# Layer 0 of a four-layer graph network: the first pair's scores ahead of the value sums, and the copy between two exponentials

## The chip, the core and the metric

The kernel runs on one core of one Trainium2 chip, in one launch. The metric is the device time in microseconds, the median of three executions. A profile of one execution, with a record of every instruction, was taken beside them. The engines are TensorE (matmuls; in the profile PE, and PEld for its weight loads), VectorE (DVE), ScalarE (ACT), GpSimd (POOL) and SyncE (SP), which issues the DMAs. Each engine works through its own instructions in order; semaphores tie them together.

## What is computed

Four layers update x (8 graphs of 1024 nodes with 128 features) one after the other. The change touches layer 0 alone, attention with 4 heads of 32 features. The 1024 keys fall into 8 chunks of 128, and each chunk has a softmax of its own:

```python
kc = k.reshape(B, H, Nc, CHUNK, Dh)
vc = v.reshape(B, H, Nc, CHUNK, Dh)
scores = jnp.einsum('bhnd,bhjcd->bhnjc', q, kc) / jnp.sqrt(jnp.asarray(Dh, dtype=q.dtype))
scores = jnp.clip(scores, -10.0, 10.0)
scores = jnp.where(mask == 0, jnp.asarray(-10.0, scores.dtype), scores)
attn = jax.nn.softmax(scores, axis=-1)
ctx = jnp.einsum('bhnjc,bhjcd->bhnd', attn, vc)
...
out = ctx @ Wo.T + bo
out = out + x
```

A layer norm and a residual follow. The input of each layer is relu(layernorm(x)). Layers 1 to 3 are other kinds of graph attention.

## The kernel before

Layer 0 runs in eight stages, one for each graph. A stage has 16 steps: two halves of 512 queries, by 8 key chunks in each (`half, jt = divmod(i, T)`). Four heads are handled in two pairs, `hp` 0 and 1. The parts of a step, by engine and by the names of the profile:

- **Scores** (`scores`, L386, and L390 in the chunks 1, 4 and 7, whose mask is added by matmuls): TensorE writes the keys x queries scores of a pair into one half of `s_ps`. It waits until the exponential has read that half (`exp_done`). There is one such buffer for each pair.
- **Exponential** (`exps`, L558): ScalarE writes a pair's exponentials to `e`. `e` has two buffers in turn, so the first exponential of step i waits for the value sums of step i-2 (`pv_done`).
- **Clip** (`clip`, L704, or L701 in the masked chunks): VectorE clips `e` in place. There are two in a step.
- **Column sums** (`sums`, L402): TensorE adds up `e` over the keys, as 32-column matmuls side by side, into `sum_ps`.
- **Value sums** (`values`, L420): TensorE multiplies `e` with the values, 4 heads side by side, into the bank `ctx_ps`. They wait for `chunk_copied` and `chunk_weighed`.
- **Copy** (`copy_chunk`, L564): ScalarE takes `ctx_ps` out into `chunk`.
- **Inverses** (`spread_inverses`, L412) and **product** (`weigh`, L725): half a stage later, TensorE spreads the inverse sums of a chunk to all rows, into the same bank `ctx_ps`, and VectorE multiplies them with the copy. Every second product is followed by an addition (L730).

So `ctx_ps` holds in turn the value sums of one chunk (written by TensorE, read by ScalarE) and the inverses of an older one (written by TensorE, read by VectorE). The order is written out by hand. At step i TensorE does: inverses of step i, column sums and value sums of step i-1, scores of step i+1. ScalarE does the copy of step i-2 and both exponentials of step i; VectorE the product, then the two clips. In between stand pieces of the next graph's projections and of the last graph's output, at fixed steps: on ScalarE, for instance, eight parts of h (L125) after step 3; on VectorE the inversion (`invert`, 2.7 us in all) between the clips of steps 0 and 8, and the residual's work after steps 2 and 14.

Stage 0 has no inverses before its step 9.

Of the kernel before, what the change touches and what calls it, by code (L numbers as in the profile page):

```python
# [177 lines left out]
def layer0(c, x_in, adj_t, w):  # L178
# [7 lines left out]
    STEPS = 2 * T  # L186
# [6 lines left out]
    with ExitStack() as ctx:  # L193
# [157 lines left out]
        def _(pe):  # L351
# [5 lines left out]
            def turn(n, par):  # L357
                if not (isinstance(n, int) and n == 0):
                    pe.wait_ge(u_ready, 2 * n - 1)
                nm.pe_turn(pe, n, par)  # L360
# [55 lines left out]
            def values(b, par, i):  # L416
                pe.wait_ge(chunk_copied, 16 * b + i + 1)
                pe.wait_ge(chunk_weighed, 16 * b + i + 1)
                for h in range(H):
                    ins = pe.matmul(ctx_ps[h * DH:(h + 1) * DH, :], v[par][:, i % T, h * DH:(h + 1) * DH],  # L420
                                    e[:, 2 * (i % 2) + h // 2, h % 2, :], start=True, stop=True,
                                    tile_position=(0, h * DH))
                ins.then_inc(pv_done, 1)
# [13 lines left out]
            def stacks(n):  # L437
                pe.wait_ge(q_stacked, STACK * (n + 1))
                pe.wait_ge(k_stacked, STACK * (n + 2))

            def stage(b, par, first, more):
                n = b + 1
                if first:
                    stacks(b)
                    for hp in range(2):
                        scores(b, par, 0, hp)
                    pe.wait_ge(v_ready, b + 1)
                for i in range(STEPS):
                    before = (b, par, i - 1) if i >= 1 else (b - 1, 1 - par, STEPS - 1)
                    after = (b, par, i + 1) if i + 1 < STEPS else (n, 1 - par, 0)  # L450
                    if first and i == 9:
                        pe.wait_ge(selected, 16)
                    if not (first and i < 9):
                        pe.wait_ge(chunk_copied, 16 * b + i)
                        spread_inverses(b, i)
                    if not (first and i == 0):
                        sums(before[0], before[2])
                        values(*before)
                    if more or i + 1 < STEPS:
                        if i + 1 == STEPS:  # L460
                            stacks(n)
                        for hp in range(2):
                            scores(*after, hp)
                    if not first and i == 1:
                        if isinstance(b, int) and b == 1:
                            pe.wait_ge(const_stored, 48)
                        output(b - 1, 0)
                    if more:
                        if i == 4:
                            turn(n, 1 - par)  # L470
                        elif i == 7:
                            q(n)
                        elif i == 9:
                            k(n)
                        elif i == 12:
                            vv(n)
                    if i == 14:
                        if more:
                            pe.wait_ge(v_ready, n + 1)
                        if not first:  # L480
                            output(b - 1, 1)

            def tail():
# [12 lines left out]
                output(B - 1, 1)  # L496

            walk(pe, prepare, stage, tail)

        @block.scalar  # L500
        def _(act):
            act.sem_inc(exp_done, 2)
            act.sem_inc(chunk_copied, 1)
            act.sem_inc(k_stacked, STACK)
            act.wait_ge(loaded, 80)

            def h_t(n):
                act.wait_ge(v_projected, n + 1)
                if not (isinstance(n, int) and n == 0):
                    act.wait_ge(x_updated, 2 * n - 1)  # L510
                nm.act_h_t(act, n)

            def high(n, projected, bias, done, free, value):
                act.wait_ge(projected, n + 1)
                act.wait_ge(free, value)
                act.activation(split[:, 0, :], aux[:, :], ACT.Identity, bias=bias[:, 0:1]).then_inc(done, 1)

            def q(n):
                high(n, q_projected, bq, q_hi, k_stacked, STACK * (n + 1))

            def k(n):
                high(n, k_projected, bk, k_hi, q_stacked, STACK * (n + 1))

            def v_out(n, par):
                act.wait_ge(v_projected, n + 2)
                act.activation(v[par][:, :, :], aux_t, ACT.Copy).then_inc(v_ready, 1)

            def normed(b, half):
                m = 2 * b + half
                act.wait_ge(offset2_done, m + 1)  # L530
                for t in range(4):
                    ins = act.activation(u[:, t, :], u[:, t, :], ACT.Identity, bias=offset2[:, t:t + 1],
                                         scale=rstd2[:, t:t + 1])
                ins.then_inc(u_normed, 1)

            def prepare(n, par):
                nm.act_h(act, n, par)
                h_t(n)
                q(n)
                k(n)  # L540
                v_out(n, par)

                act.wait_ge(prior_steps, 2)
                act.activation(pr[:, 3:4], pr[:, 2:3], ACT.Exp, scale=-1.0).then_inc(prior_ready, 1)
                act.wait_ge(late_loaded, 128)
                for x in range(16):
                    act.activation(spread[:, x // 8, x % 8, :], same_head, ACT.Copy,
                                   scale=row_is[:, x:x + 1]).then_inc(selected, 1)
                act.wait_ge(prior_ready, 1)
                act.activation(pr[:, 4:5], pr[:, 3:4], ACT.Ln, bias=c.ones[:, 0:1])  # L550
                act.activation(pr[:, 6:7], c.ones[:, 0:1], ACT.Ln, bias=pr[:, 5:6]).then_inc(prior_ready, 1)
                act.wait_ge(bounded, 3)

            def exps(b, i, hp):
                act.wait_ge(s_ready, 32 * b + 2 * i + hp + 65)
                if hp == 0:
                    act.wait_ge(pv_done, 16 * b + i + 1)
                act.activation(e[:, 2 * (i % 2) + hp, :, :], s_ps[:, hp, :, :], ACT.Exp,  # L558
                               scale=SCALE).then_inc(exp_done, 1)

            def copy_chunk(b, i):
                act.wait_ge(pv_done, 16 * b + i + 3)
                act.wait_ge(chunk_weighed, 16 * b + i + 1)
                act.activation(chunk[:, i % T, :], ctx_ps[:, :], ACT.Copy).then_inc(chunk_copied, 1)  # L564

            def stage(b, par, first, more):
                n = b + 1
                for i in range(STEPS):
                    if i >= 2:
                        copy_chunk(b, i - 2)  # L570
                    elif not first:
                        copy_chunk(b - 1, i + STEPS - 2)
                    exps(b, i, 0)
                    exps(b, i, 1)
                    if i == 0 and not (isinstance(b, int) and b < 2):
                        normed(b - 2, 1)
                    elif i == 4 and not first:
                        normed(b - 1, 0)
                    if more:
                        if i == 3:  # L580
                            if not first:
                                act.wait_ge(u_ready, 2 * b + 1)
                                act.wait_ge(late_ready, b)
                            nm.act_h(act, n, 1 - par)
                        elif i == 6:
                            h_t(n)
                        elif i == 8:
                            q(n)
                        elif i == 11:
                            k(n)  # L590
                        elif i == 13:
                            v_out(n, 1 - par)

            def tail():
                copy_chunk(B - 1, STEPS - 2)
                copy_chunk(B - 1, STEPS - 1)
                normed(B - 2, 1)
                normed(B - 1, 0)
                normed(B - 1, 1)

            act.sem_inc(pv_done, 2)
            walk(act, prepare, stage, tail)

        @block.vector
# [1411 lines left out]
```

## Time and profile before

| | |
|---|---|
| median of three executions | 2156.48 us |
| lowest and highest | 2144.48 and 2159.27 us |
| the profiled execution | 2157.34 us, of which the span of the trace 2155.5 us |
| mean granted clock of TensorE in it | 0.902 of full speed |
| busy in the span: TensorE, VectorE, ScalarE | 1736.7, 1595.2, 1346.2 us |

Layer 0 fills the span from about 57 to 749 us. Times below are microseconds from the start of the span. Matmuls are pipelined, and a row's time reaches until its last column has left; how long a group takes in a chain is the distance between its start and the start of the next. A bracket at the end of a row tells how long the engine had been idle and what it waited for. The granted clock has two levels here, 1.00 (2.4 GHz) and 0.50 (1.2 GHz).

### The profile page before, as it was taken

To read this page: it belongs to the slowest core of one execution; us is meant where nothing else is said; L and a number is where in the kernel's file an instruction comes from. 1 tells how busy PE (TensorE), PEld (TensorE's weight loads), DVE (VectorE), ACT (ScalarE), POOL (GpSimd) and SP (SyncE) were. 2 spreads that over 40 slices of the span, in tenths; PEclk is the share of its full clock that TensorE was granted. 3 is DMA by queue.
4 is the path that set the end of the run, shared out by engine and by line. 5 is a ranking of instruction groups with operands and counts; after the bars stand their busy time and mean duration, and the time that the engine had idled before them with its cause. 6 is when DMAs were issued, how large, how long until landed. Compare 5 with 4: busy or idle time off the path is not lost. (4 is left out here: it accounts for less than half of the span.)

```text
span 2155.5 us, 37200 instructions
## 1 busy us (share of the span) xinstructions
PE 1736.7 (81%) x13876; PEld 1102.1 (51%) x13876; DVE 1595.2 (74%) x2790; ACT 1346.2 (62%) x1767; POOL 111.6 (5%) x130
## 2 busy tenths in 40 slices
PE   2888888888888827699899977797877776999997
PEld 1344343443344325577677755675656553555554
DVE  2676767677767746678888889988988965767674
ACT  2665645555455517577677778988889834545553
POOL 0000000101000010000000000000000000000000
PEclk9999989999899957899999988998988988999999
DMA  6413031130311021111111112221112202000000
GB/s 191 98 40 79 1 79 40 41 79 1 79 40 40 1 82 55 35 40 50 41 40 41 50 51 70 70 70 61 61 60 70 79 26 79 11 10 20 10 10 20
DMA packets 50270, 108.92 MB, mean 51 GB/s; under 512 B 7633, under 2 KB 26450, under 8 KB 50098
## 3 DMA queue, kind: packets, MB, share of 16 engines
q1 hardware_dynamic: 50098, 106.54, 17.1%
q8 instruction: 119, 1.95, 0.4%
q14 instruction: 53, 0.43, 0.1%
HBM read 68.37 MB, written 4.59 MB: 34 GB/s over the span
## 5 line engine op out<-in xcount | busy, mean ns | idle before, releaser
L1052 ACT ACTIVATE g<-s_all,steep_d 128x1024 fp8e4<-128x1024 f32 x608 | 642.3, 1135 | 42.1 <-DMA s_all<-s_rows 26.4
L993 PE MATMUL acc<-parts,g 128*128 128x102 bf16 (+1 forms) x6144 | 418.0, 229 | 28.5 <-DVE sums L1143 19.3
L993 PEld LDWEIGHTS acc<-parts,g 128*128 128x128 fp8e4 x6144 | 401.6, 99 | 61.6 <-issue 43.8
L975 PE MATMUL post<-parts,edge 128*128 128x396 bf16 (+1 forms) x1024 | 232.9, 383 | 83.7 <-DVE base L1151 83.7
L558 ACT ACTIVATE e<-s_ps 128x1024 f32<-128x1024 f32 x256 | 248.9, 1022 | 37.0 <-PE s_ps L390 26.6
L1136 DVE TENSOR_TENSOR g<-g,edge 128x1024 int32<-128x1024 int32 x192 | 227.7, 1218 | 34.6 <-ACT g L1052 34.6
L564 ACT ACTIVATE chunk<-ctx_ps 128x512 f32<-128x512 f32 x128 | 76.2, 596 | 243.1 <-PE ctx_ps L420 243.1
L386 PE MATMUL s_ps<-qs,ks 128*128 128x512 f32 x512 | 207.4, 517 | 12.4 <-issue 7.5
L975 PEld LDWEIGHTS post<-parts,edge 128*128 128x128 fp8e4 x1024 | 102.2, 102 | 191.3 <-issue 106.6
L704 DVE SCALAR_TENSOR_TENSOR e<-e,bound 128x1024 f32<-128x1024 f32 x160 | 189.8, 1220 | 8.4 <-ACT e L558 8.4
L420 PE MATMUL ctx_ps<-e,v 128*32 128x512 f32 x1024 | 152.7, 668 | 48.8 <-DVE weighed L725 42.0
L386 PEld LDWEIGHTS s_ps<-qs,ks 128*128 128x128 f32 x512 | 102.0, 213 | 144.1 <-issue 109.1
L1830 ACT ACTIVATE z<-z,shift 128x1024 f32<-128x1024 f32 x64 | 73.6, 1150 | 160.5 <-DVE shift L1906 160.5
L1143 DVE TENSOR_REDUCE sums<-acc 128x132 f32<-128x396 f32 (+1 forms) x256 | 133.9, 566 | 28.5 <-PE acc L993 28.3
L402 PE MATMUL sum_ps<-e,pick 128*32 128x256 f32 x2048 | 146.2, 405 | 9.4 <-DVE e L704 8.8
L725 DVE TENSOR_TENSOR weighed<-chunk,ctx_ps 128x512 f32<-128x512 f32 x96 | 65.8, 686 | 96.0 <-PE ctx_ps L412 94.7
L1737 PE MATMUL s_ps<-ht,q 128*128 128x512 f32 x256 | 121.5, 597 | 4.3 <-DVE top L1899 3.2
L1899 DVE CUSTOM_DVE_ANT_0 z<-s_ps,bias 128x1024 f32<-128x1024 f32 x64 | 78.4, 1225 | 60.7 <-PE s_ps L1737 60.4
L1759 PE MATMUL o_ps<-zt,h 128*128 128x512 f32 x256 | 118.0, 605 | 6.3 <-ACT zt L1835 6.3
L125 ACT ACTIVATE h<-x,offset,rstd 128x128 f32<-128x128 f32 (+1 forms) x256 | 101.8, 482 | 31.1 <-POOL offset L118 31.1
L1126 DVE TENSOR_SCALAR g<-s_all,minus_d 128x1024 fp8e4<-128x1024 f32 x160 | 114.1, 746 | 6.0 <-DVE x L1183 2.7
L412 PE MATMUL ctx_ps<-inv_sum,spread 128*128 128x256 f32 x256 | 68.7, 352 | 48.1 <-DVE inv_sum L716 28.7
(157 smaller groups left out, 2208.8 us busy)
## 6 DMA issues: line engine op xcount, KB each, us to landing
s_all<-s_rows SPq DMA_DIRECT2D x96, 512.0 KB, 3.6
qs<-split SPq DMA_DIRECT2D x128, 128.0 KB, 2.3
ks<-split SPq DMA_DIRECT2D x128, 128.0 KB, 2.3
x<-in_x SPq DMA_DIRECT2D x8, 512.0 KB, 6.0
adj_in<-in_adj SPq DMA_DIRECT2D x8, 512.0 KB, 4.1
out_x<-x SPq DMA_DIRECT2D x8, 512.0 KB, 3.2
parts<-in_adj_t SPq DMA_DIRECT2D x6, 512.0 KB, 6.0
chunk<-in_adj_t SPq DMA_DIRECT2D x4, 512.0 KB, 6.5
```

Of the source, the lines that this page charges most:

```text
L386: ins = pe.matmul(s_ps[:, hp, j, :], ks[par][:, 2 * hp + j, jt * P:(jt + 1) * P], qs[par][:, 2 * hp + j, half * HALF:(half + 1) * HALF], s ...
L402: ins = pe.matmul(sum_ps[h * DH:(h + 1) * DH, :], pick[:, at:at + DH], e[:, 2 * (i % 2) + h // 2, h % 2, q * QUARTER:(q + 1) * QUARTER], s ...
L420: ins = pe.matmul(ctx_ps[h * DH:(h + 1) * DH, :], v[par][:, i % T, h * DH:(h + 1) * DH], e[:, 2 * (i % 2) + h // 2, h % 2, :], start=True, ...
L558: act.activation(e[:, 2 * (i % 2) + hp, :, :], s_ps[:, hp, :, :], ACT.Exp, scale=SCALE).then_inc(exp_done, 1)
L704: dve.scalar_tensor_tensor(out=tile, in0=tile, scalar=CLIP_LO, in1=lim, op0=ALU.max, op1=ALU.min).then_inc(p_ready, 1)
L975: ins = pe.matmul(self.post[:, it % 2, 0:H * 3 * W1].rearrange("p (h k c) -> p h k c", h=H, k=3), self.c.edge[:, jt, it * P:(it + 1) * P], ...
L993: ins = pe.matmul(self.acc[:, bank, o:o + self.NS], self.g[:, h % RING, jt, it * P:(it + 1) * P], self.upper[par][:, jt, h, :, :].rearrang ...
L1052: act.activation(self.g[:, h % RING, jt, :], self.s_all[:, h % 2, :], ACT.Relu, bias=self.steep_d[par][:, jt, h:h + 1], scale=STEEP, satur ...
L1136: dve.tensor_tensor(both, both, c.edge[:, some, :].rearrange("p t n -> p (t n)").bitcast(I32), ALU.bitwise_and).then_inc(self.g_ready, 1)
L1143: dve.tensor_reduce(self.sums[par][:, h, PER * k:PER * k + PER, :, :].rearrange("p i k c -> p i (k c)"), self.acc[:, (READS * h + k) % 4, ...
L1737: ins = pe.matmul(s_ps[:, j * HALF:(j + 1) * HALF], q[par][:, i * P:(i + 1) * P], ht[par][:, j * HALF:(j + 1) * HALF], start=True, stop=True)
L1759: ins = pe.matmul(o_ps[:, :], c.h[:, par, t, :], zt[:, quad, t, :], start=(t == 0), stop=(t == T - 1))
```

## The change

On TensorE, the scores of the next step are split: those of the first pair stand ahead of the value sums, those of the second behind. On ScalarE, the copy moves from the front of the first exponential to the place between the two. All instructions stay as they are, and none is added or removed; what each waits for stays too.

```diff
--- before.py
+++ after.py
@@ -455,12 +455,14 @@
                         spread_inverses(b, i)
                     if not (first and i == 0):
                         sums(before[0], before[2])
-                        values(*before)
                     if more or i + 1 < STEPS:
                         if i + 1 == STEPS:
                             stacks(n)
-                        for hp in range(2):
-                            scores(*after, hp)
+                        scores(*after, 0)
+                    if not (first and i == 0):
+                        values(*before)
+                    if more or i + 1 < STEPS:
+                        scores(*after, 1)
                     if not first and i == 1:
                         if isinstance(b, int) and b == 1:
                             pe.wait_ge(const_stored, 48)
@@ -566,11 +568,11 @@
             def stage(b, par, first, more):
                 n = b + 1
                 for i in range(STEPS):
+                    exps(b, i, 0)
                     if i >= 2:
                         copy_chunk(b, i - 2)
                     elif not first:
                         copy_chunk(b - 1, i + STEPS - 2)
-                    exps(b, i, 0)
                     exps(b, i, 1)
                     if i == 0 and not (isinstance(b, int) and b < 2):
                         normed(b - 2, 1)
```

TensorE, before: step 9 of stage 0, with the inverses (`spread`), the column sums (`sum_ps<-e,pick`), the value sums (`ctx_ps<-e,v`) and the scores (`s_ps<-qs,ks`).

```order
L412 MATMUL ctx_ps<-inv_sum,spread 128x256 [waits inverted,chunk_copied,selected]
L412 MATMUL ctx_ps<-inv_sum,spread 128x256
L402 MATMUL sum_ps<-e,pick 32x256 [waits sums_read,p_ready]
L402 MATMUL sum_ps<-e,pick 32x256 x7
L420 MATMUL ctx_ps<-e,v 32x512 [waits chunk_weighed,chunk_copied]
L420 MATMUL ctx_ps<-e,v 32x512 x3
L386 MATMUL s_ps<-qs,ks 128x512 [waits exp_done]
L386 MATMUL s_ps<-qs,ks 128x512
L386 MATMUL s_ps<-qs,ks 128x512 [waits exp_done]
L386 MATMUL s_ps<-qs,ks 128x512
```

TensorE, the same place in the changed program:

```order
L412 MATMUL ctx_ps<-inv_sum,spread 128x256 [waits inverted,chunk_copied,selected]
L412 MATMUL ctx_ps<-inv_sum,spread 128x256
L402 MATMUL sum_ps<-e,pick 32x256 [waits sums_read,p_ready]
L402 MATMUL sum_ps<-e,pick 32x256 x7
L386 MATMUL s_ps<-qs,ks 128x512 [waits exp_done]
L386 MATMUL s_ps<-qs,ks 128x512
L420 MATMUL ctx_ps<-e,v 32x512 [waits chunk_weighed,chunk_copied]
L420 MATMUL ctx_ps<-e,v 32x512 x3
L386 MATMUL s_ps<-qs,ks 128x512 [waits exp_done]
L386 MATMUL s_ps<-qs,ks 128x512
```

The two scores of the first pair have moved from behind the value sums to the front of them; their wait for `exp_done` goes with them.

ScalarE, before: steps 3 to 5 of stage 1, with the eight parts of h after step 3.

```order
L558 ACTIVATE e<-s_ps 128x1024 [waits s_ready]
L125 ACTIVATE h<-x,offset,rstd 128x128 [waits offset_done,late_ready,u_ready]
L125 ACTIVATE h<-x,offset,rstd 128x128 x7
L564 ACTIVATE chunk<-ctx_ps 128x512 [waits chunk_weighed,pv_done]
L558 ACTIVATE e<-s_ps 128x1024 [waits pv_done,s_ready]
L558 ACTIVATE e<-s_ps 128x1024 [waits s_ready]
L532 ACTIVATE h_t<-h_t,offset,rstd 128x128 [waits offset2_done]
L532 ACTIVATE h_t<-h_t,offset,rstd 128x128 x3
L564 ACTIVATE chunk<-ctx_ps 128x512 [waits chunk_weighed,pv_done]
```

ScalarE, the same place in the changed program (lines are 2 higher there):

```order
L560 ACTIVATE e<-s_ps 128x1024 [waits s_ready]
L125 ACTIVATE h<-x,offset,rstd 128x128 [waits offset_done,late_ready,u_ready]
L125 ACTIVATE h<-x,offset,rstd 128x128 x7
L560 ACTIVATE e<-s_ps 128x1024 [waits pv_done,s_ready]
L566 ACTIVATE chunk<-ctx_ps 128x512 [waits chunk_weighed,pv_done]
L560 ACTIVATE e<-s_ps 128x1024 [waits s_ready]
L534 ACTIVATE h_t<-h_t,offset,rstd 128x128 [waits offset2_done]
L534 ACTIVATE h_t<-h_t,offset,rstd 128x128 x3
L560 ACTIVATE e<-s_ps 128x1024 [waits pv_done,s_ready]
```

The copy now stands behind one exponential in each step.

## Rows read from the trace of the kernel before

**Rows 1.** Windows: busy us per engine, clock, DMA, over layer 0

```profile
57.00:749.00 692.00, 599.11 (x4448) 287.16 (x4448) 498.53 (x791) 390.63 (x518) 39.09 (x47) 0.91 0.21 47
```

**Rows 2.** Waits of layer 0 (52 to 745 us): total us, times, longest

```profile
PE ctx_ps L420 <- DVE weighed L725: 39.2, 20, 2.1
...
PE ctx_ps L412 <- ACT chunk L564: 8.1, 5, 2.8
...
PE ctx_ps L420 <- DVE ctx_sb L725: 6.6, 10, 1.1
```

**Rows 3.** Timeline of stage 3, steps 10 to 12: start, us, instruction

```profile
369.70 1.07 PE L420 MATMUL ctx_ps<-e,v 128*32 128x512 f32 x8
...
370.70 1.20 PE L386 MATMUL s_ps<-qs,ks 128*128 128x512 f32 x4
370.83 0.60 ACT L564 ACTIVATE chunk<-ctx_ps 128x512 f32<-128x512 f32 x1 [3.96 <-PE ctx_ps L420]
371.46 1.94 ACT L558 ACTIVATE e<-s_ps 128x1024 f32<-128x1024 f32 x2
...
371.73 0.39 PE L412 MATMUL ctx_ps<-inv_sum,spread 128*128 128x256 f32 x2
...
372.06 1.07 PE L402 MATMUL sum_ps<-e,pick 128*32 128x256 f32 x16
372.16 0.69 DVE L725 TENSOR_TENSOR weighed<-chunk,ctx_ps 128x512 f32<-128x512 f32 x1 [0.34 <-PE ctx_ps L412]
...
373.00 1.06 PE L420 MATMUL ctx_ps<-e,v 128*32 128x512 f32 x8
...
373.99 0.50 PE L386 MATMUL s_ps<-qs,ks 128*128 128x512 f32 x1
...
375.57 0.59 ACT L564 ACTIVATE chunk<-ctx_ps 128x512 f32<-128x512 f32 x1
...
376.21 0.50 PE L412 MATMUL ctx_ps<-inv_sum,spread 128*128 128x256 f32 x2
```

**Rows 4.** VectorE's timeline, stage 3, products 13 to 15

```profile
382.08 0.69 DVE L725 TENSOR_TENSOR weighed<-chunk,ctx_ps 128x512 f32<-128x512 f32 x1 [2.03 <-PE ctx_ps L412]
...
385.38 0.69 DVE L725 TENSOR_TENSOR weighed<-chunk,ctx_ps 128x512 f32<-128x512 f32 x1 [0.34 <-PE ctx_ps L412]
...
394.00 0.69 DVE L725 TENSOR_TENSOR weighed<-chunk,ctx_ps 128x512 f32<-128x512 f32 x1
```

**Rows 5.** Timelines of stage 1 (steps 3 to 5) and stage 4 (steps 3, 4)

```profile
146.69 1.02 ACT L558 ACTIVATE e<-s_ps 128x1024 f32<-128x1024 f32 x1
...
148.34 0.68 DVE L725 TENSOR_TENSOR weighed<-chunk,ctx_ps 128x512 f32<-128x512 f32 x1
...
149.17 1.07 PE L420 MATMUL ctx_ps<-e,v 128*32 128x512 f32 x8 [1.74 <-DVE weighed L725]
...
152.55 0.69 DVE L725 TENSOR_TENSOR weighed<-chunk,ctx_ps 128x512 f32<-128x512 f32 x1 [1.26 <-PE ctx_ps L412]
...
156.73 0.69 DVE L725 TENSOR_TENSOR weighed<-chunk,ctx_ps 128x512 f32<-128x512 f32 x1 [1.03 <-PE ctx_ps L412]
...
420.70 0.68 DVE L725 TENSOR_TENSOR weighed<-chunk,ctx_ps 128x512 f32<-128x512 f32 x1
...
426.51 0.69 DVE L725 TENSOR_TENSOR weighed<-chunk,ctx_ps 128x512 f32<-128x512 f32 x1 [2.86 <-PE ctx_ps L412]
```

**Rows 6.** Timeline cut so that only the value sums' second half shows

```profile
373.43 0.64 PE L420 MATMUL ctx_ps<-e,v 128*32 128x512 f32 x4
```

**Rows 7.** Windows: a stretch at full clock, then three at the lower level

```profile
334.00:361.00 27.00, 22.21 (x186) 10.44 (x178) 22.20 (x26) 16.72 (x22) 0.00 (x0) 1.00 0.00 1
111.90:115.30 3.40, 3.40 (x12) 1.49 (x5) 2.14 (x3) 1.25 (x3) 0.00 (x0) 0.50 0.85 193
...
422.50:425.90 3.40, 3.40 (x13) 1.52 (x9) 1.15 (x2) 1.79 (x3) 0.07 (x1) 0.50 0.00 0
...
705.80:709.20 3.40, 3.40 (x14) 1.10 (x7) 2.91 (x3) 0.88 (x2) 0.00 (x0) 0.50 0.00 0
```

## The prediction

> **What bounds the kernel now.** I read the windows first: layer 0, which the change touches, takes 692 of 2155.5 us, with TensorE busy in 599 of them and a granted clock of 0.91 [rows 1]; the other three layers keep their code. Seven full stages and a first one without inverses share the 692 us: some 89 us to a full stage, 5.6 us to a step. Then the waits [rows 2]. TensorE waits for VectorE's product before the value sums (39.2 + 6.6 us, 30 times) and hardly ever for ScalarE's copy (8.1 us, 5 times). Last the timelines, in which I follow one lap from value sums to value sums. With nothing else in the step it takes 3.30 us, from 369.70 to 373.00, and is pure TensorE work: value sums 1.00, four scores 1.03, inverses 0.33, column sums 0.94 (distances of the starts in [rows 3]). The copy starts at 370.83, as the value sums end, and lasts 0.60; it is done at 371.43, and the scores run until 371.73: hidden. Other steps are set by VectorE. A product without an idle bracket, as at 394.00 in [rows 4], follows VectorE's own work, and one with a bracket waited for TensorE. So layer 0 changes hands: after the inversion and the residual's work VectorE is late, in the steps between TensorE is.
>
> **What the new order does to a lap.** Count from the start S of the value sums. The value sums end and release ScalarE at S + 1.13 (369.70 to 370.83). Now the first exponential goes there; the instruction behind an exponential starts 0.92 later (two take 1.94 [rows 3], one 1.02 [rows 5]), so the copy starts at 2.05 and ends at 2.65. The inverses of the next step may not overwrite the bank before: 2.70 (at 375.57 + 0.59 the copy ends, at 376.21 they start, 0.05 later). TensorE has only the second pair of scores, 0.57, to fill S + 1.0 to 2.7, and stands 1.1 us. Then inverses 0.33, column sums 0.94, the first pair 0.57, and the value sums again at S + 4.54. The cover that hid the copy, a whole set of scores, is cut in half, while the copy moved 0.92 back.
>
> **Two more switches.** The second half of the eight value-sum records starts at 373.43 [rows 6], 0.43 after the first at 373.00; the scores start 0.56 after that half, so the passage from four 32-column matmuls side by side to the whole array costs 0.13. No run shows a passage back alone; the step from inverses to column sums takes 0.33 where two 256-column matmuls at the scores' rate (0.257 for 512) would take 0.26, so 0.07 bounds it below. I take 0.12 each: the new order has four passages in a step where there were two, and both new ones lie in the lap. A lap is then 4.54 + 0.24 = 4.78 us, against 3.30; where the pair is one with a mask, the lap is longer still, before and after.
> The Trainium skill (TensorEngine Tiling (Array Packing), Key Properties) says that changing the tiling mode drains TensorE. The 0.13 us agree with it; without the rule's cost the forecast below would be some 10 us less.
>
> **Stage by stage.** I go by the starts of VectorE's product [rows 4]; what lies between two products without TensorE in it stays.
> - Two steps of a stage are bare laps, product to product 3.30 (382.08 to 385.38, and 10 to 11 likewise). They become 4.78: 2 x 1.48 = +3.0.
> - From product 15 to product 0 of the next stage, the value sums follow the product directly. Before: 0.83 from product to value sums (148.34 to 149.17 [rows 5]), 1.00, two pairs 1.14, and 0.43 from inverses to product (371.73 to 372.16 [rows 3]) = 3.4 at full clock. Now the copy ends it: 0.83 + 2.70 + 0.43 = 4.0. +0.6.
> - Product 3 to 4 takes 4.21 (148.34 to 152.55 [rows 5]). ScalarE has the eight parts of h there, behind the second exponential, which the copy now delays by 0.6; the value sums wait in addition for a first pair with mask. +1.0 (between 0.6, the delay alone, and 1.3).
> - Product 4 to 5 takes 4.18 (152.55 to 156.73 [rows 5]) and becomes a lap: +0.6.
> - Five more steps are TensorE's, with a projection or a late clip in them; they carry the two switches, 0.24 each, less what the filled wait gives back: +0.7.
> - Against it: where the product comes late, the first pair is already computed when it comes. After the inversions (products 1 to 2 and 9 to 10) this shortens the road by a pair, 0.57 each: -1.1. In the other late places (2 to 3, 5 to 6, 14 to 15) VectorE's own chain goes from product to product, so that the filled wait buys nothing but the start of the next lap.
> Sum +4.8 us a stage, of which I count 4.4, since a late product 4 leaves less for the lap behind it; 7 x 4.4 = 31, and 4 for the first stage, whose second half has the same laps: **+35 us**.
>
> **The clock gives some back.** Most waits of about 2 us before the product are followed by a stretch at a granted 0.50, 1.2 GHz. Fourteen such stretches, 47.6 us, stand behind waits in steps 3, 5, 6, 11, 12 and 15 (the first, the last and one of step 3 in [rows 7]); the other fourteen, some 65 us, nearly all follow the inversion. What one costs: product 3 to 4 takes 4.21 at full clock and 5.81 at 1.2 GHz (420.70 to 426.51) [rows 5]: 1.6 us. The new order breaks each such idle time into two, one on each side of column sums and first pair, about 1 us each. From 334 to 361 us TensorE is idle 18% of the time, in pieces up to 2 us, and the granted clock stays at 1.00 [rows 7]; a bare lap of the new order idles 1.1 of 4.8 us, 23%. I expect nearly all fourteen gone: 14 x 1.5 = -21 us. The stretches behind the inversion stay, since its chain is VectorE's; there the pair set ahead saves up to another half microsecond, but the new lap can bring a low stretch of its own, and I leave both out.
>
> **Sum.** 2157.3 (the profiled execution, 0.9 above the median of the three) + 35 - 21 = 2171.3, and with 1 us for what I rounded down, **2172 us**. Its own band, by the switch at 0.07 or 0.16 and 11 to 16 low stretches gone, is 2161 to 2183.
>
> **Rivals.**
> 1. *The clock does not recover* (slower side). If the pieces of idle time, two to a step, lower the clock as the long ones did, nothing is given back: 2157 + 35 = 2192. It decides if TensorE's idle pieces, shorter but more of them, still bring the lower level. For it: waits of at most 2.1 us [rows 2] sufficed to bring 1.2 GHz at 422.50 [rows 7]. Against it: one of 1.74 at 149.17 left the clock alone [rows 5]. 0.20.
> 2. *A wash.* The switches cost nothing in the lap (-12, half a dozen to eight laps a stage at 0.24) or the low stretches behind the inversion shrink as well (65 us of them; six fewer at 1.6 give 10): 2147 to 2161. 0.27.
> 3. *The waits are simply filled.* If the copy still came in time, as at 371.43 before 371.73, the 30 waits of [rows 2] would take a first pair each: 30 x 0.7 = 21, and 21 of clock: 2115; with a part of the laps lost, 2115 to 2145. Against it: the copy needs 0.92 + 0.60 us behind an exponential and TensorE has 0.57 to bridge it. 0.08.
> That nothing happens, because the first pair waits for its bank, is ruled out: its bank is free with the previous first exponential, at S + 2.15, and the pair comes at S + 3.97 at the earliest.
> The forecast itself has 0.45.
>
> **Chances and range.** The range takes in the forecast's band, the wash and most of rival 1: 2148 to 2195. About 1% (21 us) is what a measurement of this kernel can tell from no change; the three runs of before already spread over 15 us. Slower by over 1%, above 2178: all of rival 1 and a third of the forecast, 0.36. Faster by over 1%, below 2135: 0.05. Within: 0.59.
>
> **What the profile would show.** Right: TensorE waiting for ScalarE's copy before the inverses some 60 to 80 times, about 1 us each (5 times now); its wait for the product down from 46 us to under 25; the bare lap at 4.7 to 4.9; fewer low stretches, near 14 where 28 were (65 us where 112 were), those left mostly behind the inversion; the copy directly behind the first exponential. Wrong, if the bare lap stays under 4.2, if the low stretches do not fall in number, or if anything past layer 0 differs by more than a few microseconds.

## The result and the profile after

The changed kernel takes 2185.18 us (median of four; 2182.35 to 2190.05), the kernel before 2156.07 (four). The ratio is 1.0142, with a 95% interval of 1.0117 to 1.0166: slower by 1.4%. Measured once more on another chip it was 1.0150 (1.0105 to 1.0194), 2186.31 us. The forecast was 2172 us, 1.007, within 2148 to 2195. The direction and the mechanism were right. Half of the size was missing.

The profiled execution took 2190.05 us, its span 2188.3. Layer 0's last product of all starts at 798.3 us, where it was 776.1: +22.2. What follows, the same code in both, took 1390.0 us against 1379.4. In a second profile of the changed kernel layer 0 ended at 801.6 and the rest took 1382.3. The kernel before was profiled only once, and an unprofiled execution of it took 2144.48 us, 13 less than the profiled one. So the 22 and 25 us in layer 0 are differences from one trace.

First the window over layer 0 (busy us per engine, granted clock, DMA), which answers to [rows 1]. It is 22 us longer, the granted clock is 0.97 where it was 0.91, and TensorE was busy for 609 of 714 us.

```profile
57.00:771.00 714.00, 609.39 (x4444) 264.67 (x4448) 499.15 (x790) 378.25 (x518) 40.99 (x47) 0.97 0.20 46
```

Then the waits of layer 0 (52 to 775 us; us in total, times, longest), which answer to [rows 2]. The wait for the product has gone from 45.8 us to 11.7. In its place stands the wait of the inverses (L412) for ScalarE's copy (L566): 57.3 us in 65 waits, where it was 8.1 us in 5. ScalarE's first exponential waits for the value sums, as the copy did.

```profile
ACT e L560 <- PE ctx_ps L420: 312.7, 114, 6.4
...
PE ctx_ps L412 <- ACT chunk L566: 57.3, 65, 1.8
...
PE ctx_ps L420 <- DVE weighed L727: 10.6, 8, 1.9
...
PE ctx_ps L420 <- DVE ctx_sb L727: 1.1, 3, 0.4
```

The timeline of one bare lap in stage 7 (start, length, instruction) answers to [rows 3]. From value sums to value sums it takes 757.71 - 752.86 = 4.85 us, against 3.30. The first exponential starts at 754.05, the copy 0.92 behind it, the inverses 0.64 after the copy's start, and TensorE stood idle for 1.03 us before them.

```profile
752.86 1.07 PE L420 MATMUL ctx_ps<-e,v 128*32 128x512 f32 x8
...
753.85 0.73 PE L386 MATMUL s_ps<-qs,ks 128*128 128x512 f32 x2
754.05 1.03 ACT L560 ACTIVATE e<-s_ps 128x1024 f32<-128x1024 f32 x1 [2.42 <-PE ctx_ps L420]
754.97 0.59 ACT L566 ACTIVATE chunk<-ctx_ps 128x512 f32<-128x512 f32 x1
755.44 1.03 ACT L560 ACTIVATE e<-s_ps 128x1024 f32<-128x1024 f32 x1
...
755.61 0.51 PE L412 MATMUL ctx_ps<-inv_sum,spread 128*128 128x256 f32 x2 [1.03 <-ACT chunk L566]
...
756.05 1.07 PE L402 MATMUL sum_ps<-e,pick 128*32 128x256 f32 x16
...
757.05 0.73 PE L386 MATMUL s_ps<-qs,ks 128*128 128x512 f32 x2
...
757.71 1.06 PE L420 MATMUL ctx_ps<-e,v 128*32 128x512 f32 x8
```

VectorE's products in stage 7, to be read as [rows 4]. First the changed kernel's products 10 to 14, 4.9, 5.3, 4.9 and 4.9 us apart:

```profile
741.13 0.69 DVE L727 TENSOR_TENSOR ctx_sb<-chunk,ctx_ps 128x512 f32<-128x512 f32 x1 [4.77 <-PE ctx_ps L412]
...
745.99 0.69 DVE L727 TENSOR_TENSOR weighed<-chunk,ctx_ps 128x512 f32<-128x512 f32 x1 [1.90 <-PE ctx_ps L412]
...
751.30 0.69 DVE L727 TENSOR_TENSOR weighed<-chunk,ctx_ps 128x512 f32<-128x512 f32 x1 [2.35 <-PE ctx_ps L412]
...
756.15 0.69 DVE L727 TENSOR_TENSOR weighed<-chunk,ctx_ps 128x512 f32<-128x512 f32 x1 [1.71 <-PE ctx_ps L412]
...
761.01 0.69 DVE L727 TENSOR_TENSOR weighed<-chunk,ctx_ps 128x512 f32<-128x512 f32 x1 [1.89 <-PE ctx_ps L412]
```

and the kernel before's products 11 to 14, 4.2, 3.3 and 3.3 us apart:

```profile
728.29 0.69 DVE L725 TENSOR_TENSOR weighed<-chunk,ctx_ps 128x512 f32<-128x512 f32 x1 [0.34 <-PE ctx_ps L412]
...
732.51 0.69 DVE L725 TENSOR_TENSOR weighed<-chunk,ctx_ps 128x512 f32<-128x512 f32 x1 [1.26 <-PE ctx_ps L412]
...
735.81 0.69 DVE L725 TENSOR_TENSOR weighed<-chunk,ctx_ps 128x512 f32<-128x512 f32 x1
...
739.11 0.69 DVE L725 TENSOR_TENSOR weighed<-chunk,ctx_ps 128x512 f32<-128x512 f32 x1 [0.35 <-PE ctx_ps L412]
```

The mean distance of a product from the one before it, over stages 1 to 6, worked out from the starts in both traces (us; those that moved by less than 0.05 are left out):

| product | before | after | |
|---|---|---|---|
| 0 | 4.07 | 4.46 | +0.38 |
| 2 | 7.09 | 5.79 | -1.30 |
| 4 | 5.00 | 4.89 | -0.11 |
| 5 | 4.24 | 4.89 | +0.64 |
| 7 | 4.80 | 4.56 | -0.24 |
| 8 | 5.03 | 5.21 | +0.18 |
| 10 | 6.56 | 5.64 | -0.92 |
| 11 | 3.30 | 4.82 | +1.52 |
| 12 | 5.48 | 5.76 | +0.29 |
| 13 | 5.62 | 5.41 | -0.21 |
| 14 | 3.30 | 4.75 | +1.45 |
| 15 | 8.61 | 8.88 | +0.27 |

The products 1, 3, 6 and 9, whose start VectorE's own work sets, did not move at all.

### The profile page after: what moved, and what is told of

Same layout as the page of the kernel before. It is cut to its first block and busy times, and to the rows that moved or that the text cites. A ratio compares the mean times of both kernels' runs of the same rounds, so it can differ in the third digit from the quotient of the medians.

```text
span 2188.3 us, 37144 instructions
## 1 busy us (share of the span) xinstructions
PE 1754.2 (80%) x13876; PEld 1087.5 (50%) x13876; DVE 1596.3 (73%) x2790; ACT 1334.5 (61%) x1767; POOL 113.0 (5%) x130
## 5 line engine op out<-in xcount | busy, mean ns | idle before, releaser
L560 ACT ACTIVATE e<-s_ps 128x1024 f32<-128x1024 f32 x256 | 263.0, 1028 | 314.8 <-PE ctx_ps L420 312.7
L386 PE MATMUL s_ps<-qs,ks 128*128 128x512 f32 x512 | 216.5, 498 | 13.2 <-issue 8.0
L386 PEld LDWEIGHTS s_ps<-qs,ks 128*128 128x128 f32 x512 | 88.0, 197 | 179.0 <-issue 174.9
L420 PE MATMUL ctx_ps<-e,v 128*32 128x512 f32 x1024 | 141.1, 623 | 11.8 <-DVE weighed L727 10.6
L412 PE MATMUL ctx_ps<-inv_sum,spread 128*128 128x256 f32 x256 | 69.0, 352 | 97.4 <-ACT chunk L566 57.3
L412 PEld LDWEIGHTS ctx_ps<-inv_sum,spread 128*128 128x128 f32 x256 | 40.5, 194 | 136.6 <-ACT chunk L566 84.3
```

The lines of the kernel that those rows point to most:

```text
L386: ins = pe.matmul(s_ps[:, hp, j, :], ks[par][:, 2 * hp + j, jt * P:(jt + 1) * P], qs[par][:, 2 * hp + j, half * HALF:(half + 1) * HALF], s ...
```

## The experiments

S is again the start of the value sums in a lap. Each kernel was run beside the kernel before on the same chip. "Low stretch" stands for a stretch at a granted clock of 0.50.

| kernel | median us | before | ratio (95%) | layer 0 ends | low clock in layer 0 |
|---|---|---|---|---|---|
| before | 2156.07 | | | 776.1 | 113 us, 28 stretches |
| changed | 2185.18 | 2156.07 | 1.0142 (1.0117 to 1.0166) | 798.3 | 34, 9 |
| changed again | 2186.31 | 2149.71 | 1.0150 (1.0105 to 1.0194) | 801.6 | 51, 11 |
| 1 TensorE's part alone | 2148.65 | 2153.50 | 0.9972 (0.9948 to 0.9996) | 767.5 | 44, 12 |
| 2 ScalarE's part alone | 2192.22 | 2153.50 | 1.0162 (1.0132 to 1.0191) | 815.3 | 72, 15 |
| 3 pair ahead of column sums | 2166.41 | 2153.50 | 1.0052 (1.0033 to 1.0072) | 785.4 | 44, 13 |
| 4 copy last | 2304.42 | 2153.50 | 1.0669 (1.0630 to 1.0707) | 918.9 | 150, 40 |
| 5 pair early in late steps only | 2136.57 | 2158.72 | 0.9898 (0.9872 to 0.9924) | 748.1 | 55, 13 |
| 6 scores ahead of inverses | 2141.22 | 2158.72 | 0.9928 (0.9907 to 0.9948) | 759.2 | 61, 14 |
| 7 both | 2126.29 | 2158.72 | 0.9857 (0.9833 to 0.9881) | 741.1 | 27, 7 |
| 8 four scores early | 2135.12 | 2158.72 | 0.9888 (0.9868 to 0.9909) | 752.0 | 51, 12 |
| 9 k a step later | 2104.42 | 2149.71 | 0.9766 (0.9724 to 0.9809) | 721.1 | 17, 3 |

"Layer 0 ends" is the start of its last product in the one profiled execution. The last column has the time at a granted 0.50, added up along that trace from 65 us to the start of the last value sums, and the number of its stretches. Only the changed kernel was profiled twice, the others once.

**1. TensorE's part alone.** The first hunk of the diff without the second.

```diff
-                        values(*before)
...
+                        scores(*after, 0)
+                    if not (first and i == 0):
+                        values(*before)
+                    if more or i + 1 < STEPS:
+                        scores(*after, 1)
```

> TensorE's part of the change alone: the first pair's scores ahead of the value sums, the copy at its old place ahead of both exponentials. Theory A (the copy behind an exponential gates the inverses): the copy ends at S + 1.73, the inverses start at S + 1.78, and a bare lap is 1.78 + 0.33 + 0.94 + 0.57 and two switches of 0.12, 3.9 us, where the changed kernel has 4.85 and the kernel before 3.30. The waits for the product are filled and most low stretches of the clock behind them go (some 20 us). Time 2150, between 2135 and 2160. Theory B (the split of the scores on TensorE is what costs: switches, and value sums that stand behind a pair): as slow as the changed kernel, 2180 or more.

Measured 0.9972, 2148.65, which is the time of theory A; theory B is refuted. The timeline of a bare lap in stage 7:

```profile
723.50 0.73 PE L386 MATMUL s_ps<-qs,ks 128*128 128x512 f32 x2
...
724.16 1.07 PE L420 MATMUL ctx_ps<-e,v 128*32 128x512 f32 x8
...
725.29 0.60 ACT L566 ACTIVATE chunk<-ctx_ps 128x512 f32<-128x512 f32 x1 [1.59 <-PE ctx_ps L420]
725.78 1.93 ACT L560 ACTIVATE e<-s_ps 128x1024 f32<-128x1024 f32 x2
...
725.95 0.50 PE L412 MATMUL ctx_ps<-inv_sum,spread 128*128 128x256 f32 x2
...
728.04 1.06 PE L420 MATMUL ctx_ps<-e,v 128*32 128x512 f32 x8
```

The copy starts at S + 1.13, the inverses at S + 1.79, the next value sums at S + 3.88 (3.86 expected). So the split of the scores by itself costs a bare lap 0.6 us (3.88 against 3.30) and wins that back, and a little more, in the steps with a late product.

**2. ScalarE's part alone.** The second hunk without the first.

```diff
+                    exps(b, i, 0)
                     if i >= 2:
                         copy_chunk(b, i - 2)
                     elif not first:
                         copy_chunk(b - 1, i + STEPS - 2)
-                    exps(b, i, 0)
                     exps(b, i, 1)
```

> ScalarE's part alone: the copy between the two exponentials, all four scores behind the value sums as before. Theory A: the first exponential waits for the first pair, S + 1.67, the copy ends at S + 3.2, the inverses start at S + 3.25; a bare lap is 4.5 us against 3.30, and no wait for the product is filled, so that the low stretches of the clock stay about as before (110 us in layer 0). Time 2190, between 2178 and 2205, slower than the whole change or equal to it. Theory B: the copy's place costs nothing, 2157.

Measured 1.0162, 2192.22, and a bare lap of 4.71 us (4.5 expected):

```profile
769.75 1.06 PE L420 MATMUL ctx_ps<-e,v 128*32 128x512 f32 x8
770.74 0.76 PEld L386 LDWEIGHTS s_ps<-qs,ks 128*128 128x128 f32 x4 [0.84 <-issue]
...
771.51 1.02 ACT L558 ACTIVATE e<-s_ps 128x1024 f32<-128x1024 f32 x1 [2.27 <-PE s_ps L386]
772.43 0.59 ACT L564 ACTIVATE chunk<-ctx_ps 128x512 f32<-128x512 f32 x1
...
773.08 0.51 PE L412 MATMUL ctx_ps<-inv_sum,spread 128*128 128x256 f32 x2 [1.13 <-ACT chunk L564]
...
774.46 1.06 PE L420 MATMUL ctx_ps<-e,v 128*32 128x512 f32 x8
```

The exponential comes at S + 1.76, not 1.67, since it waits until the first pair has left TensorE. The copy's new place costs 1.6% by itself, and on top of TensorE's part 1.7 points (1.0142 against 0.9972). With or without the split, the loss is the copy's. One expectation failed: the low stretches were to stay at some 110 us and came to 72 in 15. The waits for the product had shrunk from 45.8 to about 30 us without being filled.

**3. The pair ahead of the column sums too.** Two passages between the whole array and the 32-column matmuls in a step, not four. The edit is against the changed kernel: the column sums move behind the pair.

```diff
-                    if not (first and i == 0):
-                        sums(before[0], before[2])
                     if more or i + 1 < STEPS:
                         if i + 1 == STEPS:
...
                         scores(*after, 0)
                     if not (first and i == 0):
+                        sums(before[0], before[2])
                         values(*before)
```

> As the changed kernel, but the first pair's scores stand ahead of the column sums too, right behind the inverses, so that TensorE passes between the whole array and 32-column matmuls twice in a step, as in the kernel before, and not four times. If the switches cost 0.12 to 0.15 us each in the lap, a bare lap goes from 4.85 to about 4.55, and the whole from 2185 to about 2168 (2160 to 2176). If a switch costs nothing, the lap stays at 4.85 and the time at 2185.

Measured 2166.41; the bare lap went from 4.85 to 4.52. Two passages less are worth 0.33 us in a lap that TensorE and the copy set in turn, 0.16 each, and 20 us in the kernel. The order of these groups was changed with the number of passages, so the 0.16 holds both, and no run separates them. The Trainium skill (TensorEngine Tiling (Array Packing), Key Properties) says that a change of the tiling mode drains TensorE, without a price; the 0.16 agrees with it.

**4. The copy last.** A second dose: the copy stands behind both exponentials. The edit is against the changed kernel.

```diff
                     exps(b, i, 0)
+                    exps(b, i, 1)
                     if i >= 2:
                         copy_chunk(b, i - 2)
                     elif not first:
                         copy_chunk(b - 1, i + STEPS - 2)
-                    exps(b, i, 1)
```

> As the changed kernel, but the copy stands behind both exponentials. A second dose of the suspected cost. Theory A: the copy and with it the inverses come 0.92 us later in every lap, a bare lap goes from 4.85 to 5.8, and some 70 to 90 copy waits grow by 0.9 each: 2250 (2235 to 2275). If the copy does not gate the lap, the time stays near 2185.

Measured 2304.42, above the expected range. The wait for the copy grew as foreseen: 82 waits and 122.0 us up to 775 us, against 65 and 57.3. Up to 895 us, where layer 0 ends here, it is:

```profile
PE ctx_ps L412 <- ACT chunk L566: 147.5, 96, 2.3
```

and the bare laps of stages 1 to 6 went to 5.7. What was not foreseen is the clock: 40 low stretches, 150 us, where the changed kernel has 9 and 34. With about 2 us of idle time in a lap (5.7 less 3.5 of TensorE's own work) the low clock of rival 1 is there. The right base for the doses is experiment 1, which has the same order on TensorE and the copy first. From it the bare lap goes from 3.88 to 4.85 and to 5.7, nearly the same step twice, but the time from 0.9972 to 1.0142 and to 1.0669: 1.7 points and then 5.3. The price is not proportional to the dose. How much of the second is the clock was not separated.

**5. The pair early only where the product is late.** ScalarE as before.

```diff
+                    early = i in (1, 3, 6, 9, 15)
                     if not (first and i == 0):
                         sums(before[0], before[2])
-                        values(*before)
+                        if not early:
+                            values(*before)
...
-                        for hp in range(2):
-                            scores(*after, hp)
+                        scores(*after, 0)
+                    if early and not (first and i == 0):
+                        values(*before)
+                    if more or i + 1 < STEPS:
+                        scores(*after, 1)
```

> The copy stays ahead of both exponentials, and the first pair goes ahead of the value sums only in the steps 1, 3, 6, 9 and 15, where TensorE waits for a late product; all other steps are as in the kernel before. If the waits are worth filling and the bare laps are what the split costs, the bare laps stay at 3.30 us, products 2, 4, 7, 10 and 0 come 0.6 to 1.4 us earlier each as in TensorE's part alone, and nothing is lost elsewhere: some 4 us a stage, 2125 (2112 to 2140). If the gain of the filled waits is given back by ScalarE or by the stacks' DMAs, it stays within 1% of TensorE's part alone, 2149.

Measured 0.9898, 2136.57, inside the range: 22 us between the medians where 31 were expected. Layer 0 of the profiled execution ended 28 us earlier (748.1 against 776.1). The bare laps are back at 3.30, the mean distance to product 4 fell from 5.00 to 3.42 and to 7 from 4.80 to 4.13. Some of the gain went at product 12, which came after 6.07 us where it came after 5.48, 0.6 us in the mean of six stages.

**6. All four scores ahead of the inverses in steps 1 and 9,** where these wait for the inversion.

```diff
+                            for hp in pairs:
+                                scores(*after, hp)
...
+                    place = "inverses" if i in (1, 9) else "pair" if i in () else "four" if i in () else "behind"
+                    if place == "inverses":
+                        next_scores(0, 1)
                     if not (first and i < 9):
                         pe.wait_ge(chunk_copied, 16 * b + i)
```

> As the kernel before, but in steps 1 and 9 all four scores stand ahead of the inverses, which wait there for the inversion on VectorE (25.7 us in 14 waits), so that TensorE works through that wait. If the low clock behind the inversion comes from this idle time, most of the low stretches at steps 0, 1, 8 and 9 go (some 65 us of them), and products 2 and 10 come 1.1 us earlier for the scores and about 1.5 for the clock: 2130 (2118 to 2145). If the low clock has another cause, the scores alone give 16 us: 2140, with the stretches still there.

Measured 0.9928, 2141.22: inside the range of the first expectation, though its clock was to go lower and 2140 was the figure of the second. The scores run in the gap, and the inverses follow them (stage 3, step 1):

```profile
310.62 0.73 PE L386 MATMUL s_ps<-qs,ks 128*128 128x512 f32 x2 [0.27 <-ACT e L572]
...
311.54 0.74 PE L386 MATMUL s_ps<-qs,ks 128*128 128x512 f32 x2 [0.18 <-ACT e L572]
...
312.11 0.40 PE L412 MATMUL ctx_ps<-inv_sum,spread 128*128 128x256 f32 x2
...
314.10 0.67 DVE L739 TENSOR_TENSOR ctx_sb<-chunk,ctx_ps 128x512 f32<-128x512 f32 x1
```

Product 2 comes 2.1 us earlier (7.09 to 4.96), product 10 2.5 (6.56 to 4.08). Of the 14 low stretches that began behind product 0, 1, 8 or 9 two are left, so most of the low clock there did come with this idle time. But 7 now begin behind product 11 or 12, where 3 did, and product 12 takes 7.96 us where it took 5.48.

**7. Both** (steps 1 and 9 as in 6, first pair ahead of the value sums in 3, 6 and 15).

> Both: all four scores ahead of the inverses in steps 1 and 9, the first pair ahead of the value sums in steps 3, 6 and 15, all else as before, the copy first. The two gains should add, since they stand in different steps: 2115 (2100 to 2130).

Measured 0.9857, 2126.29, inside the range. Product 12 takes 8.06 us, and the timeline of stage 3 shows why:

```profile
360.02 1.11 ACT L530 ACTIVATE split<-aux,bk 128x1024 fp32r<-128x1024 f32 x1 [4.46 <-DMA qs<-split]
361.03 0.59 ACT L578 ACTIVATE chunk<-ctx_ps 128x512 f32<-128x512 f32 x1
...
361.67 0.79 PE L412 MATMUL ctx_ps<-inv_sum,spread 128*128 128x256 f32 x2 [3.41 <-ACT chunk L578]
```

ScalarE waits 4.46 us for the DMAs that stack q before it may overwrite `split`, the copy stands behind that instruction, and the inverses waited 3.41 us for the copy.

**8. As 7, with all four scores ahead of the value sums in steps 3, 6 and 15.**

> As the one with both, but in steps 3, 6 and 15 all four scores stand ahead of the value sums. The wait for the product there is about 2 us, four scores take 1.1 to 1.8, and one set of scores keeps TensorE at two switches a step. The copy is then covered by nothing and the inverses start at S + 1.78 instead of S + 2.1 or more: 3 to 8 us less than with the first pair, 2108 (2095 to 2125).

Measured 0.9888, 2135.12, above the range and 9 us slower than 7: the expectation failed. VectorE sets products 4 and 7 in both (3.39 and 4.13 us against 3.42 and 4.13), so there was nothing left to win. Product 8 takes 5.72 against 5.18 and product 13 6.90 against 6.13, with 5 more low stretches. The inverses' wait for the copy went from 24.0 us in 9 waits to 39.2 in 29: with all four scores ahead, none is left to cover the copy. Whether that accounts for the whole loss was not settled.

**9. k a step later.** As 7, and the instruction of ScalarE that waits for the stacking DMAs (it overwrites `split` for the next graph's k), VectorE's part of k, and v behind them, one step later. The excerpt has ScalarE's part; TensorE's `vv` moves from step 12 to 13 and VectorE's `low` for k from 11 to 12.

```diff
-                        elif i == 11:
+                        elif i == 12:
                             k(n)
-                        elif i == 13:
+                        elif i == 14:
                             v_out(n, 1 - par)
```

> As the one with all four scores ahead of the inverses and the first pair ahead of the value sums in steps 3, 6 and 15, and besides ScalarE's and VectorE's part of the next graph's k projection one step later (12 instead of 11), its v projection in step 13 and v's copy in step 14. In the kernel with both, ScalarE stands 4.46 us at step 11 for the DMAs that stack q, with the copy behind it, and product 12 comes after 8.0 us where 4.2 to 5.5 would do; the clock is low behind it in six stages. If this DMA wait is what takes back part of the gain there, product 12 comes 3 us earlier and its low stretches go: 7 x 3 and some 8 of clock, 2100 (2092 to 2112). If what is saved there is lost at step 14, where v must be ready before the output, the time stays within 8 us of 2126.

Measured 0.9766 (0.9724 to 0.9809), 2104.42 us: 2.3% faster than the kernel before and 3.7% faster than the changed one. ScalarE's wait for the DMAs (us, times, longest), first in the kernel with both, then here:

```profile
ACT split L530 <- DMA qs<-split: 30.5, 7, 4.9
```

```profile
ACT split L530 <- DMA qs<-split: 3.3, 5, 0.9
```

Product 12 comes after 4.22 us instead of 8.06, and 3 low stretches are left. Product 13 comes after 4.26 us instead of 6.13, and product 14 gives back 1.8 us (3.30 to 5.07).

**The changed kernel again.**

> The changed kernel once more, for a second profile of it and a ratio from another chip: layer 0 ends near 798 us again, its bare lap is 4.85, and the time 2180 to 2190. What follows layer 0, the same code, took 10.6 us longer in the first profile; if that is chance of the clock, it lies anywhere between 1379 and 1392 here.

The bare lap is 4.85 again, and the rest after layer 0 took 1382.3 us. Layer 0 ended at 801.6, 3.3 us later than in the first profile. Over the twelve profiles the rest behind layer 0, the same code in each, took between 1379.4 and 1391.9. So the 10.6 us more in the first profile of the changed kernel lie within the spread, and what the traces show of the change is the 22 to 25 us in layer 0. The ratios, 1.0142 and 1.0150, make it some 31 us; with one profile of the kernel before, that gap is not explained.

## Why the prediction held, and where its size was off

The forecast was +15 us on the profiled execution, a sum of +35 for the laps and -21 for the clock; the medians are 29 us apart. The way and the mechanism came true: the copy gates the lap, and part of the clock comes back.

**The lap.** Forecast 4.78, measured 4.85. By terms, with the forecast in brackets: value sums to exponential 1.19 (1.13), exponential to copy 0.92 (0.92), copy to inverses 0.64 (0.65), inverses to column sums 0.44 (0.33), column sums to the pair 1.00 (1.06 with a switch), pair to value sums 0.66 (0.69 with a switch). Above their time without a passage (0.94 and 0.57) the two new passages, priced at 0.12 each, show as 0.06 and 0.09, and another 0.11 lies between the inverses and the column sums, behind the idle time. The sum came out nearly right by errors that offset each other. Experiments 1, 2 and 4 show that the place of the copy is what gates the lap.

**The TensorE waits.** 65 waits of 0.9 us for the copy against 60 to 80 of about 1; 11.7 us for the product against under 25. Both held.

**The steps of a stage.** +1.52 and +1.45 at the bare laps (1.48 forecast), +0.64 at product 5 (+0.6). Product 4 took 4.6 to 5.0 where it had taken 4.2 at full clock: +0.4 to +0.8 (+1.0 forecast). The mean of product 0 went up by 0.38 and not by 0.6. Products 2 and 10 gained 1.30 and 0.92, of which 0.57 each was forecast as work; the rest goes with the clock, which was low there less often, though no run separates the two.

**The term that was mis-sized** is "7 x 4.4": it takes the last stage for one like the others. Stages 1 to 6 together, from product 0 of stage 1 to product 0 of stage 7, went from 542.0 to 552.1 us, +1.7 a stage, where 4.4 - 3 = 1.4 was forecast, and the first stage gave +4.2 where 4 was forecast. What is left, the last stage with the tail of layer 0, went from 105.5 to 113.5: +8.0 where the sum has 1.4. It prepares no further graph, so the projections that fill some steps of the others are missing, and it has five bare laps (products 5, 8, 11, 13 and 14), each 1.55 longer. This could have been read from the trace of before, products 728.29 to 739.11 above. It is 6.6 of the 8 us by which layer 0 came out above the forecast in the first profile. With it the sum for layer 0 would have read 21 us, against 22.2 and 25.5 measured. The rest of the 29 us between the medians can lie in the spread of the layers behind it, or in that of layer 0 itself, which ended 3 us later in the second profile; the runs do not tell these apart. One sign of being wrong did show in the first profile: what lies past layer 0 differed by 10.6 us, more than the "few microseconds" that the prediction allowed. The twelve profiles show that this bound was too tight for code that had not changed.

**The clock.** The number of low stretches was to fall from 28 to about 14, their time to 65 us. It fell to 9 and 34 (11 and 51 in the second profile), since some of those behind the inversion went too. By 1.6 us a stretch that would give back 27 to 30 us rather than 21, yet the time did not come back in full. In stages 3 and 4 of the changed kernel the clock was never low. Product 10 came 4.5 us after the one before, and product 12 after 6.5; in stages 1 and 2, with a low clock behind step 8, it was 5.9 and 5.3, nearly the same sum. Stage 3, and below it ScalarE's same instruction in stage 3 of the kernel before:

```profile
377.87 0.69 DVE L727 TENSOR_TENSOR weighed<-chunk,ctx_ps 128x512 f32<-128x512 f32 x1 [1.84 <-PE ctx_ps L412]
...
381.24 1.11 ACT L518 ACTIVATE split<-aux,bk 128x1024 fp32r<-128x1024 f32 x1 [3.04 <-DMA qs<-split]
...
383.15 0.60 ACT L566 ACTIVATE chunk<-ctx_ps 128x512 f32<-128x512 f32 x1
...
384.34 0.69 DVE L727 TENSOR_TENSOR weighed<-chunk,ctx_ps 128x512 f32<-128x512 f32 x1 [0.67 <-PE ctx_ps L412]
```

```profile
374.56 1.11 ACT L516 ACTIVATE split<-aux,bk 128x1024 fp32r<-128x1024 f32 x1 [1.16 <-DMA qs<-split]
```

ScalarE stood 3.04 us for the stacking DMAs, with the first exponential and the copy of step 12 behind it. What is won at product 10 is waited for at product 12. The prediction had not priced that the DMAs of q have a length of their own. In all twelve traces the sixteen of a stage take 11.8 to 13.4 us from the first issue, at about product 9, to the last landing; 9.4 to 11.1 us of that lie between SyncE's first issue and its last. The kernel before waited for them too (14.6 us in 6 waits; the changed one 14.2 in 6), and a gain in the steps beside them is cut there. The stretch from product 9 to product 12 shows it. By the mean distances it takes 15.3 us in the kernel before, 16.2 in the changed one, 15.2 to 15.4 in experiments 1, 5, 6, 7 and 8, which all have the copy first, and 11.6 only in 9. In 6 and 7 ScalarE's wait grows to 30 us, and the gain appears once the waiting instruction is moved. It was not moved in the changed kernel itself, so for that one this part of the account is argued, not shown.

**The rivals.** The clock recovered, so rival 1 was wrong for this change, though in experiment 4, with one more microsecond of idle time in a lap, it did not. Rival 2 had one half right: the low stretches behind the inversion did shrink in number. But the switches were not free (0.16 us each in experiment 3), and the laps took more than the clock gave. The filled waits of rival 3 were real: 34 of 46 us went. It failed at the copy, as stated. Experiment 5 keeps the copy first and fills only these waits, and wins 1.0%.

## What to carry to other kernels

When a bank is shared by a writer and two readers, and the writer waits for it in every lap, try first to put the instruction that empties it ahead in its engine's queue. Here each 0.9 us of other work put ahead of it came back as 0.9 to 1.0 us of idle time in a bare lap, and the second dose cost three times the first (5.3 points against 1.7), with the low clock back in 40 stretches. Work that fills a wait should be moved only in the steps that have the wait; here the same edit was worth 0.3% when done in every step, and 1.0% in five of 16 steps. Before multiplying a gain or a loss per stage, look at the first and the last stage, and at the one DMA chain that may set the pace as soon as the engines do not.

## What the runs showed that I had not expected

- The DMAs that stack q set the pace of steps 10 to 12, by the 15.3 us above already in the kernel before: with the copy first, other orders of TensorE's work moved the wait and not the sum. They kept ScalarE for up to 4.9 us, and moving the instruction that waits for them, with the rest of k and v, by one step was worth 0.9 points (0.9857 to 0.9766, each against the kernel before on its own chip).
- Code that did not change (layers 1 to 3) takes 1379 to 1392 us from profile to profile, 0.6% of the whole, in step with the granted clock: 0.90 over that stretch in the kernel before, 0.89 in the first profile of the changed one. A difference of 10 us in the total of one execution is no evidence on layer 0. The end of layer 0 in the trace is better, but it moved by 3 us between the two profiles of the changed kernel.
